# A gated attention layer with a mixture of experts: the experts placed between two halves of the attention, a batch's values in one PSUM bank, maxima of 1024 columns

## The reference

```
q = xn @ Wq.T (16 heads of 8);  k = xn @ Wk.T, v = xn @ Wv.T (one head of 8, shared)
s = softmax(q k^T * scale) v  @ Wout.T                      # per batch and head
t = rmsnorm(xn) * norm_scale;  logits = t @ gate_w + gate_b
two best of 8 experts per token, weights = softmax of the two
y = sum over the two of w * ((swiglu(t @ w1 + b1)) @ w2 + b2)   # 128 -> 512 -> 256 -> 128
f = xn + y;  out = x + s * silu(f)
```

## Time and profile before

| | us |
|---|---|
| median of 3 runs | 492.01 (491.53 to 496.53) |
| the profiled execution's time | 495.04 |
| its span, first to last instruction | 493.3 |

### The profile page before, as it was taken

The page is one execution under the profiler, slowest core; times in us unless marked ns, Lnnn a source line. Parts: engine busy times, 40 slices in busy tenths (PEclk is TensorE's granted clock), DMA queues, the critical chain, the costliest instruction groups (busy, mean ns, idle before and its releaser), DMA issues. The chain is left out here.

```text
span 493.3 us, 9961 instructions
## 1 busy us (share of the span) xinstructions
PE 391.6 (79%) x2484; PEld 241.3 (49%) x2514; DVE 350.1 (71%) x882; ACT 272.0 (55%) x598; POOL 272.9 (55%) x459
## 2 busy tenths in 40 slices
PE   0975577789999999999999997599999999990000
PEld 0653132343444454444444542389999999980000
DVE  5974996797978888898889870066666666650993
ACT  1451154466777777777777776166666666650210
POOL 9587740028777767777784000017777767773552
PEclk9996558799999999999999999699999999996555
DMA  7133149214222222222222103046665656623742
GB/s 189 33 104 100 57 147 387 82 41 151 84 85 75 84 78 82 70 89 83 79 84 82 57 6 107 15 115 163 177 176 165 177 169 178 172 88 123 231 125 64
DMA packets 48887, 56.41 MB, mean 114 GB/s; under 512 B 14291, under 2 KB 36947, under 8 KB 48726
## 3 DMA queue, kind: packets, MB, share of 16 engines
q1 hardware_dynamic: 42646, 43.29, 29.6%
q0 software_dynamic: 5632, 12.66, 7.6%
q10 hardware_dynamic: 576, 0.08, 0.1%
HBM read 32.83 MB, written 20.08 MB: 107 GB/s over the span
## 5 line engine op out<-in xcount | busy, mean ns | idle before, releaser
L1150 DVE TENSOR_REDUCE maxes<-ps 128x2 f32<-128x512 f32 x256 | 168.5, 679 | 39.8 <-PE ps L748 38.9
L593 ACT ACTIVATE probs<-ps 128x512 f32<-128x512 f32 x256 | 139.5, 588 | 38.1 <-PE ps L734 32.4
L507 POOL DMA_INDIRECT y_dram<-ys,xs x80 | 85.1, 1064 | 99.2 <-ACT ys L666 64.0
L748 PE MATMUL ps<-k_max,qs 96*128 96x256 bf16 x512 | 105.5, 291 | 20.2 <-DVE maxes L1150 11.4
L734 PE MATMUL ps<-qs,k_exp 128*128 128x512 bf16 x226 | 89.2, 399 | 4.0 <-DMA qs<-m_T 3.0
L480 POOL DMA_INDIRECT sorted_dram<-row_st,pos_st x64 | 65.0, 1016 | 32.0 <-POOL row_st L476 21.1
L856 PE MATMUL ps<-xT,w_st 128*128 128x256 f32 x320 | 77.7, 387 | 4.0 <-issue 3.3
L748 PEld LDWEIGHTS ps<-k_max,qs 96*128 96x128 bf16 x512 | 47.2, 102 | 61.1 <-DVE maxes L1150 30.8
L763 PE MATMUL ps<-probs,v_use 128*32 128x512 f32 x512 | 71.5, 634 | 2.0 <-DVE s_all L1032 1.0
L1186 DVE TENSOR_SCALAR probs<-ps,b_st 128x256 f32<-128x256 f32 x80 | 35.0, 480 | 50.9 <-PE ps L856 43.3
L856 PEld LDWEIGHTS ps<-xT,w_st 128*128 128x128 f32 x320 | 58.8, 194 | 11.1 <-issue 3.8
(11 more groups left out here) (150 smaller groups left out, 493.8 us busy)
## 6 DMA issues: line engine op xcount, KB each, us to landing
w_st<-in_w SPq DMA_DIRECT2D x40, 256.0 KB
qs<-q_dram SPq DMA_DIRECT2D x32, 288.0 KB
sorted_dram<-pad_row SPq DMA_DIRECT2D x2, 2600.0 KB, 11.5
xs<-sorted_dram SPq DMA_DIRECT2D x40, 130.0 KB, 2.4
q_all<-y_dram SPq DMA_DIRECT2D x8, 512.0 KB, 4.8
q_dram<-q_parts POOLq DMA_DIRECT2D x16, 192.0 KB, 3.0
x_all<-in_x SPq DMA_DIRECT2D x4, 512.0 KB, 7.0
out<-x_all SPq DMA_DIRECT2D x8, 256.0 KB, 2.3
```

The lines of the kernel that those rows point to most:

```text
L507: gp.indirect_dma_start(out=y_dram, out_offset=bass.IndirectOffsetOnAxis(ap=at[:, t, :], axis=0), in_=ys[:, r, t, :], in_offset=None).then ...
L593: sc.activation(probs[:, n % 2, k, :], ex_bank[BANKS[n % 2][k]], ACT.Exp).then_inc(m["exp_ok"], 1)
L748: last = te.matmul(mx_bank[bank][:, e * S:(e + 1) * S], qs[0:MROW, n % 4, at:at + P], k_max[0:MROW, (n // 2) % 2, :], start=True, stop=True)
L1150: ve.tensor_reduce(maxes[:, n % 2, st, 2 * j:2 * j + 2], mx_bank[BANKS[n % 2][k]].rearrange("p (e t) -> p e t", e=2), AX, ALU.max).then_in ...
```

## The change

It touches nearly every part.

- **Order.** `sequence` places all 40 expert blocks between unit 15 and unit 16 of the attention. The maxima run three units ahead (`AHEAD`), with six slots of q.
- **Maxima.** Two neighbouring banks are reduced by one DVE instruction (1024 columns, four a unit, negated by it); there are two such double banks. `split_m` runs once a batch, in four operations, and `turn_m` once a batch.
- **PSUM.** Three banks are a ring through which exp scores and the small transposes and projections of attention pass in a fixed order (a list of the items says which bank is whose); one bank holds the values of a batch: both units add into it, with v placed in other columns. Copy, turning and `normalise` are done once a batch.
- **Keys and values** are read where they were made, not copied by DMA for each batch; the matmuls contract over 72 and 75 rows, not 96 and 128.
- **Rows of the experts** are written by ACT (`fill_row`), two per token, all kept in SBUF, so POOL only issues the 64 scatters. The norm scale is applied in the copy behind the transpose.
- **Bias of the second expert layer**: one matmul of 256 columns for two of 128.
- **The gated sum** is formed batch by batch in the units 17 to 33: POOL does six additions and products of 256 columns for a batch, ACT the tanh at the end of the unit `tanh_step` gives, SP loads and stores. x is loaded a second time. DVE does the last two batches' final operations.
- **The start**: x in six DMAs, nine chunks instead of eight groups; DVE normalises the first four tiles, POOL the other 28; DVE splits q of the first two chunks, POOL the rest; SP writes it.

```diff
-MROW = 96
+KALL = KROWS + 3
+AHEAD = 3
+QS = 6
...
+def tanh_step(i):
+    return EXPERTS_AT + 2 + (3 * i) // 4
...
+        def sequence(attend, expert):
+            for u in range(-AHEAD, UNITS + 2):
+                if u == EXPERTS_AT:
+                    for q in range(-1, BLOCKS + 2):
+                        expert(q)
+                attend(u)
...
+            def load_m(b):
+                sp.wait_ge(m["mT_sb"], b + 1)
+                for c in range(2):
+                    sp.dma_start(qs[KROWS:KALL, (2 * b + c) % QS, :], m_T[3 * HU * c:3 * HU * (c + 1), b % 2, :]
+                                 ).then_inc(m_in[b % 2], 16)
...
+            def load_y(i):
+                if i >= YB:
+                    sp.wait_ge(m["f_ok"], i - YB + 1)
...
+            def attend(u):
+                if u == EXPERTS_AT:
+                    for r in range(4):
+                        sp.wait_ge(y_out[r], 16 * SORTED // Y_SLOTS)
+                    for i in range(YB):
+                        load_y(i)
+                    sp.dma_start(x_all[:, :, :], xv).then_inc(m["xr_in"], 16)
...
+                if 4 <= u + 5 < UNITS:
+                    load_q(u + 5)
+                if u >= -1 and u % 2 == 1 and (u + 1) // 2 < B:
+                    load_m((u + 1) // 2)
...
+            def scatter(t):
+                pool.wait_ge(m["row_ok"], t + 1)
                 for k in range(TOPK):
...
+                    gp.indirect_dma_start(out=sorted_dram, out_offset=bass.IndirectOffsetOnAxis(ap=pos_i[:, t, k:k + 1], axis=0),
+                                          in_=rows[:, t, k, :], in_offset=None).then_inc(m["scat"], 16)
+            for i in range(2, len(CHUNKS)):
+                norm(i)
...
+            for i in range(2, len(CHUNKS)):
+                split_q(i)
+            pool.wait_ge(m["route_ok"], 1)
+            pool.wait_ge(m["p_ok"], 2)
+            pool.wait_ge(m["pad_in"], 32)
+            for t in range(TILES):
+                scatter(t)
...
+            def add_second(i):
+                pool.wait_ge(m["f1_ok"], i + 1)
+                gp.tensor_tensor(xn_all[:, 2 * i:2 * i + 2, :], xn_all[:, 2 * i:2 * i + 2, :], yb[:, i % YB, :, D:2 * D], ALU.add
+                                 ).then_inc(m["f_ok"], 1)
...
+            def gate_product(i):
+                pool.wait_ge(m["th_ok"], i + 1)
+                pool.wait_ge(m["f_ok"], i + 1)
+                gp.tensor_tensor(th[:, i % 3, :], th[:, i % 3, :], tokens(xn_all, i), ALU.mult).then_inc(m["gm_ok"], 1)
...
+            def gated(b):
+                pool.wait_ge(m["g_ok"], b + 1)
+                pool.wait_ge(m["s_ok"], b + 1)
+                gp.tensor_tensor(tokens(xn_all, b), tokens(xn_all, b), s_b[:, b % 8, :], ALU.mult).then_inc(m["so_ok"], 1)
...
+            for i in range(B + 2):
+                if i < B:
+                    add_first(i)
+                if 1 <= i <= B:
+                    gate_product(i - 1)
+                if 0 <= i - 2 < POOL_OUT:
+                    gated(i - 2)
+                if i < B:
+                    add_second(i)
+                if 1 <= i <= B:
+                    gate_sum(i - 1)
+                if 0 <= i - 2 < POOL_OUT:
+                    add_x(i - 2)
...
+            def fill_row(t):
+                if t == 0:
+                    act.wait_ge(m["r_ok"], 1)
+                    act.wait_ge(m["xp_ok"], TILES - 4)
+                sc.activation(rows[:, t, :, 0:D], replicated(xn_all[:, t, :], TOPK, 1), ACT.Copy,
+                              scale=rms[:, t:t + 1]).then_inc(m["row_ok"], 1)
...
+            def gate_tanh(i):
+                act.wait_ge(m["f_ok"], i + 1)
+                if i >= 3:
+                    act.wait_ge(m["g_ok"], i - 2)
+                sc.activation(th[:, i % 3, :], xn_all[:, 2 * i:2 * i + 2, :].rearrange("p t d -> p (t d)"), ACT.Tanh,
+                              scale=0.5).then_inc(m["th_ok"], 1)
...
+                    evac_keys(2)
+                    for t in range(12, 24):
+                        fill_row(t)
+                if u == -1:
+                    evac_mT(0)
+                    evac_keys(3)
+                    evac_keys(4)
...
+            def scores_max(u, k):
+                st, j, n = k // 4, k % 4, 4 * u + k // 2
+                b = u // 2
...
+                if k % 2 == 0 and n >= 2:
+                    pe.wait_ge(m["max_ok"], n - 1)
-                    last = te.matmul(mx_bank[bank][:, e * S:(e + 1) * S], qs[0:MROW, n % 4, at:at + P],
-                                     k_max[0:MROW, (n // 2) % 2, :], start=True, stop=True)
-                last.then_inc(m["max_ps"], 1)
...
+                    last = te.matmul(ps[:, 3 + 2 * (n % 2) + k % 2, e * S:(e + 1) * S], qs[0:KROWS, u % QS, at:at + P],
+                                     k_stack[0:KROWS, b * S:(b + 1) * S], start=True, stop=True)
+                if k % 2 == 1:
+                    last.then_inc(m["max_ps"], 1)
...
+            def values(u):
+                b, c = u // 2, u % 2
+                pe.wait_ge(m["exp_ok"], CH * u + CH)
+                if c == 0 and b >= 1:
+                    pe.wait_ge(m["on_ok"], b)
...
+                for tt in range(2):
+                    for j in range(4):
+                        last = te.matmul(pv_bank[32 * j:32 * j + 32, :], v_all[:, 2 * b + tt, 16 - 16 * c:48 - 16 * c],
+                                         probs[:, u % 2, 4 * tt + j, :], start=(c == 0 and tt == 0), stop=(c == 1 and tt == 1))
+                last.then_inc(m["pv_ok"], 1)
...
+            def attend(u):
+                if u == EXPERTS_AT:
+                    pe.wait_ge(m["xsT_sb"], BLOCKS)
+                    pe.wait_ge(m["y_ok"], 2 * BLOCKS)
...
+                    if u % 2 == 0 and u >= 2:
+                        if k == VALUES_AT[0]:
+                            values(u - 1)
+                        if k == TURN_O_AT:
+                            turn_o(u // 2 - 1)
+                    if u % 2 == 1 and u > 0:
+                        if k == MT_AT and (u + 1) // 2 < B:
+                            turn_m((u + 1) // 2)
+                        if k == VALUES_AT[1] and u < UNITS:
+                            values(u - 1)
+                        if k == ONT_AT and u >= 3:
+                            turn_on((u - 3) // 2)
+                        if k == PROJECT_AT and u >= 3:
+                            project((u - 3) // 2)
...
+                    te.matmul(ps[:, bank, 0:2 * D], ones_b[:, :], replicated(bias_rows[:, bass.ds(e * D, D)], 2, 1),
+                              start=True, stop=False)
-                        yt = ps[:, 4 + 3 * (v % 2), t * D:(t + 1) * D]
-                        te.matmul(yt, ones_b[:, :], bias_rows[:, bass.ds(e * D, D)], start=True, stop=False)
+                        yt = ps[:, bank, t * D:(t + 1) * D]
...
+            def normalise(b):
+                r = b % 2
+                ov = pv_bank.rearrange("p (i j d) -> p i j d", i=4, j=8)
...
+                ve.reciprocal(inv[:, r, :, :], ov[:, :, :, DK]).then_inc(m["inv_ok"], 1)
+                dve.wait_ge(m["inv_ok"], b + 1)
...
+                ve.tensor_tensor(o_n[:, r, :, :].rearrange("p i (j d) -> p i j d", j=8), ov[:, :, :, 0:DK],
+                                 replicated(inv[:, r, :, :], DK, 3), ALU.mult).then_inc(m["on_ok"], 1)
...
+            def split_m(b):
...
+                dve.wait_ge(m["max_ok"], 8 * b + 8)
+                if b >= 2:
+                    dve.wait_ge(m["mT_ps"], b - 1)
+                ve.tensor_copy(part[0], all_neg).then_inc(m["mpart"], 1)
+                dve.wait_ge(m["mpart"], 4 * b + 1)
+                ve.tensor_tensor(part[1], all_neg, part[0], ALU.subtract).then_inc(m["mpart"], 1)
+                ve.tensor_tensor(rest, all_neg, part[0], ALU.subtract).then_inc(m["mpart"], 1)
+                dve.wait_ge(m["mpart"], 4 * b + 3)
+                ve.tensor_tensor(part[2], rest, part[1], ALU.subtract).then_inc(m["mpart"], 1)
...
+            def reduce_max(u, r):
+                b, c, n = u // 2, u % 2, 4 * u + r
+                st, h = r // 2, HU * c + 4 * (r % 2)
+                dve.wait_ge(m["max_ps"], n + 1)
...
+                ve.tensor_reduce(neg[:, b % 2, st, h:h + 4],
+                                 ps[:, 3 + 2 * (n % 2):5 + 2 * (n % 2), :].rearrange("p a (e t) -> p (a e) t", e=2),
+                                 AX, ALU.max, negate=True).then_inc(m["max_ok"], 1)
...
+            def attend(u):
+                if u == -3:
+                    dve.wait_ge(m["rms_ok"], 1)
+                    ve.reciprocal(rms, lnb[:, 5, :]).then_inc(m["r_ok"], 1)
+                    dve.wait_ge(m["r_ok"], 1)
+                if u >= -1 and u % 2 == 1 and (u + 1) // 2 < B:
+                    split_m((u + 1) // 2)
...
+                for r in range(4):
+                    if u + AHEAD < UNITS:
+                        reduce_max(u + AHEAD, r)
+                    if u == -3 and r == 0:
+                        key_rows(1)
```

(10 more changed lines are left out.)

1231 lines of the change are left out of this document (551 added, 680 removed).

## The result

| | before | after |
|---|---|---|
| median of 4 runs, us | 494.27 (491.53 to 496.79) | 511.76 (509.43 to 512.68) |
| span of the profiled execution | 493.3 | 507.5 |
| mean granted TensorE clock | 0.895 | 0.866 |

What follows compares the result with a forecast made beforehand. PE was taken to bound attention (97% busy) and experts (100%), with 49 us behind them PE-idle. Start -7, attention with hand-over +3, experts -2 and end -33 made -39: 452 us, range 430 to 472.

Steps and rivals of the forecast that it cites:

- Second half: Attention behind the experts: 120 us to the last exp at 438, with 1 for table load and 5 for POOL contention.
- Start: Kernel's beginning, normalisation mostly on POOL, smaller chunks: first maxima at 33 us, first exp at 58.5, 7 earlier.
- Unit pace: Attention units: PE and DVE wait in turn, 7.5 us a unit; bounds 6.2 and 7.9.
- The walk: Hand-stepped PE and DVE timeline of two attention units: 15.2 us a pair, values' 2 us not covered by two buffers.
- N and M: DVE's normalisation (0.7 us) and split of m (0.75) in attention; PE's turning of m waits for both, 1.45.
- The reduction: DVE's maxima over 1024 columns: 1.17 us each, saving 0.4 us of DVE a unit.
- The m DMA: Transfer of m in attention: off the path, landing at 6.3 us where PE needs it at 6.8.
- Scatters: POOL's 64 row scatters beside the first half of attention: 82 to 87 us, ending at 185 to 190.
- rival 2: Scatters or hand-over to the experts cost more: at 1.6 us a scatter +20, so 470 us; chance 0.13.
- Rival 1: Attention's waits hide and PE alone sets the pace: 6.3 to 6.8 us a unit, 438 to 442; chance 0.24.
- Rival 4: ACT switches tables between exp and tanh in the second half: 31 us, half hidden, 467; chance 0.04.
- Rival 3: POOL's gated sums bound the second half, operations of 1.5 us instead of 0.65: slower than before, 497 and more; chance 0.03.

Runs made afterwards that it cites:

- e4: Changed kernel with POOL's six gated-sum operations done on 8 of 256 columns; 492.5 us.
- e6: Changed kernel with SP loading unit 17's q and m before waiting for the last y and issuing y and x; total not used, restarted pair 16.3 us.
- e2: Changed kernel with six idle matmuls of 512 columns added before PE's wait for the split of m; 512.4 us, ratio 1.035.
- e5: Changed kernel with a unit's 16 values matmuls issued as two eights with chunks between; total not used, pairs 14.8 to 17.9 us.
- e14: e13 with a unit's 16 values matmuls issued as two eights; 458.0 us.
- e8: Changed kernel with maxima four units ahead instead of three, m split and turned earlier; total not used, undisturbed first-half pairs 13.6 us.
- e13: Changed kernel with maxima four ahead, q and m first at the restart, normalisation on DVE, experts behind 18 units, seven q slots; 457.1 us, ratio 0.929.
- e12: Changed kernel with maxima of 512 columns in four single banks, eight reductions a unit; 501.6 us, ratio 1.016.
- e16: e13 with maxima of 512 columns in four single banks; total not used, first-half pairs 12.8 us.
- e1: Changed kernel with the split of m put ahead of the previous batch's normalisation on DVE; 501.1 us, ratio 1.013.
- e7: Changed kernel with all 32 start normalisations on DVE; total not used, first maxima 42.2 us, first exp 66.6.
- e3: Changed kernel with only the reload of x moved behind the loads of unit 17; 507.1 us, ratio 1.028.
- e17: e13 with the normalisation of chunks 2 to 8 back on POOL; 568.1 us in a disturbed group, total not used.

## Why the prediction was wrong, step by step

The end was to give 33 us and gave 39 (9.7 us behind the last exp, for 48.7 behind the last ys before). All that stands ahead of it was to give 6 and cost 53. The steps that failed most are *Second half* (contention priced at 5 us, where e4 shows 17, and the restart at 1 for a table load, where e6 shows 13 to 14) and *Start*; *Unit pace* had the right waits at the wrong clock.

- **The clock.** Every step of the sum but one took the engines at their speed of before. The clock of 1.00 in the earlier trace rows was read where PE was 97% busy. The walk itself put a wait of PE for 1.45 us of DVE's work into each pair and went on counting 2 us for values; behind the wait most take 2.9 to 3.5. e2 shows the term: about 0.9 us a pair in the first half.
- **Unit pace.** The structure was right: N and M together take 1.45 (170.86 to 172.32), PE waits 1.07 for them, a pair at full clock takes 15.4 with the filling for the 15.0 to 15.2 forecast. What was wrong is the sentence that the values' 2 us are what two buffers do not cover: cutting them in two gains nothing (e5, e14), taking away the wait in front of them, and m's late landing with it, gains 2.7 a pair (e8, e13).
- **The reduction** took 1.22 for 1.17. The step "it saves 0.4 us of DVE a unit" failed not in its size but in what it left out: a buffer twice as long is returned half as often, and that costs PE more (e12, e16).
- **The m DMA** "is off that path" held by 0.5 us in the walk; in the trace it is late in two pairs of the first half (0.96 and 0.79), in e1 by up to 2.98. At the restart it was late by 11.2, and the forecast did not walk SP's queue there.
- **Contention in the second half**, forecast 0.8 a pair by half a block, was 1.6 in an ordinary pair (split 2.4 for 0.75), nearer to the 2.1 of the whole block that was priced beside it, and 4.0 in the worst, plus the clock behind the longer wait: e4 gives 17 us over five pairs, with ACT's waits for POOL in them. The Trainium skill (SBUF — State Buffer, Who interferes with whom) has the other side fully block, and names casts among what can contend; the trace agrees that a cast of 32 columns is held up, but the section has the block last for one instruction of the other side, and here it was 4.19 us, six of them. The forecast had priced the subtractions alone, and each with at most one POOL operation; the earlier trace rows had shown only such cases. The same section says that on this chip reductions never contend: they kept 1.21 to 1.23 us beside POOL.
- **Start.** Mis-sized: the sum never priced the normalisation on POOL, where it takes 0.79 us a tile, 3.1 a chunk for a PE pitch of 2.17, and waits 11.9 us for DVE's statistics. But it is not the cause of the first maxima's 9.3 us: with all of it on DVE (e7) they come at 42.2. There PE's transposes of a chunk take 1.1 us until 31.5 with a pitch of 4.6, and 2.17 had been read where they take 0.63; what slows them was not tried. Behind the first maxima e7 gains 3.4 us by the first exp. The two sets of key rows, estimated at 2 each, took 4.7 and 3.8. From the first exp to the choice it took 51.1 for 44.5, with a clock of 0.61 from 60 to 110 us, and DVE stood 4.3 us for PE's ranks; no experiment was made on them.
- **Scatters** were right (1.26 each), and rival 2 falls for them, but not for its second half: the hand-over took 15.3 us from the last scatter for at most 8: behind the last m, at 206.3, SP reads the choice and issues three weights before the first rows, at 213.95, and PE waits 5.8 for these.
- **Experts** 124.1 for 125, and the **end** 9.7 for 16: right, and better. From the last result to the end of the span it is 2.3 us (505.2 to 507.5), not 7.
- **Rivals.** Rival 1 (12.6 to 13.6 a pair) falls for this kernel, and e13, without the waits, reaches its upper end. Rival 4 falls: from the experts on ACT loads tables only at 220.2 and 342.2 us, none at a tanh. Rival 3 was on the right side with the wrong cause: POOL's operations took 0.72, not 1.5, and POOL waited for ACT's tanh 65 us. A chance of 0.03 for slower came from asking only what makes POOL the bound, and not what each of five small waits does to the same few engines.

Of the 53.5 us between forecast and trace, the experiments account for: restart 13 to 14, contention 17 to 19, the clock in the first half some 5 (hidden there in part by the scatters), reductions 8 to 10, normalisation some 3. They overlap, and the rest, the 9 us up to the first maxima among it, was not separated.

## What to carry to other kernels

A wait of one us on the busiest engine cost two here: look at the granted clock and at the duration of the same matmuls behind the wait, and lay the dependent step a unit earlier before saving instructions. Work put under another engine's stage is priced by the small dependent operations that it delays, so first take those off the path. Where a program starts a stage again, walk the in-order queue line by line: 24 KB waited for 2 MB.

## What the runs showed that was not expected

- Six matmuls added to a gap of 1.07 us cost nothing: 512.4 for 511.8 us, at a granted clock of 1.00 for 0.91.
- A DVE cast of 32 columns lasted through six POOL operations that followed each other at 0.68 us without a gap, to the end of a run of 18. The same split's cast takes 4.2 to 4.9 us in e1, e2, e3 and e12, while the casts of the changed kernel's other pairs take 0.33 to 0.78 beside such operations. So the wait was not bounded by one instruction of the other side; why there alone is not shown.
- An issue of 288 KB by SP took 5.3 us, and one in e3 9.7, while large transfers were under way (0.73 otherwise), and held all that SP had behind it.
- In the two disturbed groups PE, DVE and ACT stood for long stretches with nothing to wait for that the trace names, from the first scatters until past their end. PE's waits in e6:

```profile
PE ps L769 <- issue: 39.2, 6, 27.2
```

  It is the time in which POOL issues its scatters at the usual 1.26 us. The kernel before lost 18 to 24 us in these groups, which speaks for a condition that the whole group met; e17 took 568.1 us where e13, which differs by the normalisation alone, took 457.1. The traces list one transfer of instructions between 120 and 200 us in e6, six in the changed kernel; whether late instructions are the cause, and whether the written-out units (before, they were a loop) are why the new order loses more, was not tried and stays open.
